# Weighting the routed rows of a mixture-of-experts layer before the down product, and adding them by the gathers

## The reference, cut to what matters

```python
xn = _layernorm(x)
scores = softmax(xn @ gate_w.T)                        # 64 experts
topk_w, topk_ids = top_k(scores, 6)                    # normalised to sum 1
comb = zeros(T, 64).at[token, topk_ids].add(topk_w)
g, u = split(einsum('th,efh->tef', xn, w_gate_up))     # 176 each
act = silu(g) * u * comb[:, :, None]
routed = einsum('tef,ehf->th', act, w_down)
shared = (silu(xn @ sg) * (xn @ su)) @ ws_down         # 2 shared experts
out = x + attention(xn) @ Wo + bo + routed + shared
```

## Time and profile before

| | |
|---|---|
| three runs | 660.39, 662.77, 664.65 us; median 662.77 |
| the profiled execution | 666.26 us, its span 664.4, mean granted clock 0.997 |
| busy in the span | PE 625.2 us (94%), DVE 437.2 (66%), POOL 360.4 (54%), ACT 308.0 (46%) |
| DMA | 124.52 MB, mean 187 GB/s |

### The profile page before, as it was taken

The page is one execution under the profiler, slowest core; times in us unless marked ns, Lnnn a source line. Parts: engine busy times, 40 slices in busy tenths (PEclk is TensorE's granted clock), DMA queues, the critical chain, the costliest instruction groups (busy, mean ns, idle before and its releaser), DMA issues.

```text
span 664.4 us, 17821 instructions
## 1 busy us (share of the span) xinstructions
PE 625.2 (94%) x4928; PEld 368.9 (56%) x4929; DVE 437.2 (66%) x1328; ACT 308.0 (46%) x798; POOL 360.4 (54%) x376
## 2 busy tenths in 40 slices
PE   6999999988989999899999989999999999999997
PEld 3644455654455555555555555555554666666654
DVE  6768678456474766656566575654446688898864
ACT  3653121033343444444444444454445767777752
POOL 3000000278685877868787686874300766666662
PEclk9999999999899999999999999999999999999999
DMA  8600011238869789796887969987425777777432
GB/s 272 189 32 1 0 34 33 94 95 269 264 183 264 243 250 286 211 325 200 261 281 228 307 198 298 286 251 163 98 58 190 213 217 228 221 219 222 130 103 74
DMA packets 78167, 124.52 MB, mean 187 GB/s; under 512 B 11113, under 2 KB 52618, under 8 KB 78090
## 3 DMA queue, kind: packets, MB, share of 16 engines
q1 hardware_dynamic: 43098, 60.18, 29.4%
q0 software_dynamic: 15872, 46.16, 24.5%
q10 hardware_dynamic: 19120, 17.18, 7.7%
HBM read 85.73 MB, written 37.75 MB: 186 GB/s over the span
## 4 chain that ended last, share of the span: by engine, by line
PE 78%; DVE 5%; issue 4%; ACT 4%; POOL 3%; DMA 3%; ACTq 2%; SPq 0%; DVEq 0%; POOLq 0%
PE pair L1181 22%; PE pair L1208 15%; PE pair L1151 6%; PE pair L1138 4%; PE pair L1086 4%; PE bank L1293 4%; PE bank L1192 3%; PE bank L1165 3%; PE bank L1325 2%; PE pair L1048 2%; DVE negm L950 2%; ACTq L616 2%; PE pair L1248 2%; PE pair L1267 1%; PE bank L1304 1%
## 5 line engine op out<-in xcount | busy, mean ns | idle before, releaser
L453 POOL DMA_INDIRECT lower<-xn_rows,idx_all x128 | 134.0, 1047 | 194.8 <-DVE idx_all L925 107.2
L1181 PE MATMUL pair<-space,work 128*64 (+1 forms) x768 | 167.3, 466 | 12.0 <-ACT work L601 7.6
L1208 PE MATMUL pair<-lower,work 88*64 x512 | 123.1, 380 | 5.2 <-ACT lower L614 2.7
L1181 PEld LDWEIGHTS pair<-space,work 128*64 128x64 f32 x768 | 67.4, 138 | 84.6 <-issue 63.4
L869 DVE TENSOR_TENSOR work<-work,pair 128x176 f32<-128x176 f32 x128 | 42.5, 337 | 105.2 <-ACT work L608 104.4
L1208 PEld LDWEIGHTS pair<-lower,work 88*64 88x64 f32 x512 | 68.7, 136 | 55.5 <-issue 22.6
L1181 PE MATMUL pair<-wqkv_sb,work 128*64 128x352 f32 x256 | 90.6, 477 | 0.0
L614 ACT ACTIVATE lower<-pair 128x256 f32<-128x256 f32 x128 | 49.2, 384 | 79.7 <-PE pair L1208 79.7
L518 POOL DMA_INDIRECT wqkv_sb<-y_rows,slot_i x48 | 47.2, 984 | 60.9 <-DVE negm L950 34.0
L601 ACT ACTIVATE work<-pair 128x256 f32<-128x256 f32 x128 | 42.4, 381 | 69.0 <-PE pair L1138 39.9
L950 DVE TENSOR_REDUCE negm<-pair 128x2 f32<-128x256 f32 (+1 forms) x128 | 64.9, 551 | 11.4 <-PE pair L1256 10.2
(11 more groups left out here) (198 smaller groups left out, 1199.8 us busy)
## 6 DMA issues: line engine op xcount, KB each, us to landing
space<-wgu SPq DMA_DIRECT2D x66, 352.0 KB
y_rows<-lower ACTq DMA_DIRECT2D x128, 128.0 KB, 4.0
qk_all<-qk_rows SPq DMA_DIRECT2D x64, 256.0 KB, 4.2
lower<-wdn SPq DMA_DIRECT2D x64, 176.0 KB
qk_rows<-qk_all POOLq DMA_DIRECT2D x32, 256.0 KB
qk_rows<-space POOLq DMA_DIRECT2D x16, 256.0 KB
xn_rows<-qk_all SPq DMA_DIRECT2D x16, 128.0 KB, 2.0
lower<-xn_rows,idx_all POOLq DMA_INDIRECT x128
```

Source lines behind the costliest of these rows:

```text
L453: po.indirect_dma_start(xg[:, r % XB, :], None, xn_rows[:, :], bass.IndirectOffsetOnAxis(idx_all[:, r:r + 1], 0)).then_inc(xg_in[r % XB], 16)
L1181: last = pe.matmul(pair[u % 2][strip, 0:2 * F], xgT[u][:, c, strip], n, start=c == 0, stop=c == EC - 1, skip_group_check=True)
L1208: last = pe.matmul(pair[u % 2][strip, 512:512 + E], hT[:, u % 2, c, strip], n, start=c == 0, stop=c == 1, skip_group_check=True)
```

## The change

A row's weight is applied to the hidden values of its tile, before the down product, instead of to its result afterwards. The rows of `xn_rows` become 64 columns wider; SP writes the token's 64 weights (`comb`, one for each expert) into these columns, and a gather brings 320 columns instead of 256. `take_weights` on DVE copies, for a tile, each strip's column of the gathered weights into one column of `wcol`: it loads the first strip's expert number into a register, waits for the gather, and makes one copy of 64 x 1 for each strip. The column then scales the rows in `hidden`, which becomes a scalar_tensor_tensor. A gather now also waits until the tile four before has had its weights taken.

`slot_weights`, `w6`, `combine` and the buffers `yg` go. In the attention POOL's gathers add into `x_all` themselves (`compute_op=ALU.add`): 96 as before, in groups of four token tiles, k by k; each waits for the add before it on the same tile (`summed`). `residual` waits for the adds of its two token tiles.

```diff
-    xn_rows = nc.dram_tensor("xn_rows", (T, E), F32, kind="Internal").ap()
+    xn_rows = nc.dram_tensor("xn_rows", (T, E + NE), F32, kind="Internal").ap()
...
+            sp.wait_ge(comb_ok, 1)
+            sp.dma_start(xn_rows.rearrange("(t p) e -> p t e", p=P)[:, :, E:E + NE], comb[:]).then_inc(comb_out, 16)
...
                 if r >= XB:
                     po.wait_ge(xt_done, r - XB + 1)
+                    po.wait_ge(taken, r - XB + 1)
...
-            def rows(t, u):
...
-                    if t >= 2:
-                        po.wait_ge(dcomb, TOPK * (t - 2) + k + 1)
-                    po.indirect_dma_start(yg[u][:, k, :], None, y_rows[:, :],
-                                          bass.IndirectOffsetOnAxis(slot_i[:, t, k:k + 1], 0)).then_inc(yg_in[u], 16)
+            def add_rows(t, k, paced):
...
+                before = t // GATHERED * TOPK + k
+                if before:
+                    po.wait_ge(summed[t % GATHERED], 16 * before)
+                po.indirect_dma_start(x_all[:, t], None, y_rows[:, :], bass.IndirectOffsetOnAxis(slot_i[:, t, k:k + 1], 0),
+                                      compute_op=ALU.add).then_inc(summed[t % GATHERED], 16)
...
-                dve.tensor_tensor(hid[:, u % 2], sg[:, u % 2], pair[u % 2][:, F:2 * F], ALU.mult).then_inc(hid_ok, 1)
...
+                dve.wait_ge(taken, i + 1)
+                dve.scalar_tensor_tensor(hid[:, u % 2], sg[:, u % 2], wcol[:, i % WEIGHTS:i % WEIGHTS + 1], pair[u % 2][:, F:2 * F],
+                                         ALU.mult, ALU.mult).then_inc(hid_ok, 1)
...
+            def take_weights(i, u):
+
+                dve.reg_load(low_reg[u], tile_e[0:1, 0, bass.ds(i, 1)])
+                dve.wait_ge(xg_in[u], 16 * (i // XB + 1))
+                for g, e in enumerate((dve.snap(low_reg[u], min_val=0, max_val=XT - 1) & (P - 1), own_of(u))):
+                    strip = slice(g * GRAIN, (g + 1) * GRAIN)
+                    last = dve.tensor_copy(wcol[strip, i % WEIGHTS:i % WEIGHTS + 1], xg[strip, u, bass.ds(e + (E - SHARED), 1)])
+                last.then_inc(taken, 1)
...
             for i in range(2):
                 up_copy(i, i)
+            for i in range(XB):
+                take_weights(i, i)
...
-                if 0 <= i // 2 < PAIRS * NT:
-                    slot_weights(i // 2)
+                for n in (i + XB, i + XB + 1):
+                    if XB <= n < TILES:
+                        take_weights(n, n % XB)
...
-                dve.wait_ge(dcomb, TOPK * SB * (b + 1))
+                for t in range(SB * b, SB * (b + 1)):
+                    dve.wait_ge(summed[t % GATHERED], 16 * TOPK * (t // GATHERED + 1))
```

More of the change, by code:

```diff
@@ L60 @@
 AHEAD = 9
+WEIGHTS = 16
+GATHERED = 4
 FILL = AHEAD + 2
@@ L203, in build @@
         npad = sb("npad", [P, SB, P])
-        w6 = sb("w6", [P, NT, 8])
+        wcol = sb("wcol", [P, WEIGHTS])
         cnt = sb("cnt", [NE, 1])
@@ L275, in build @@
         tiled = sem("tiled"); placed = sem("placed"); passed_ok = sem("passed_ok"); ended = sem("ended")
-        tables_ok = sem("tables_ok"); onehot_ok = sem("onehot_ok"); listed = sem("listed"); idx_ok = sem("idx_ok"); dpair = sem("dpair")
+        tables_ok = sem("tables_ok"); onehot_ok = sem("onehot_ok"); listed = sem("listed"); idx_ok = sem("idx_ok"); comb_ok = sem("comb_ok"); comb_out = sem("comb_out"); taken = sem("taken")
         w_loaded = [sem("w_loaded_even"), sem("w_loaded_odd")]
@@ L293, in build @@
         ot_ok = sem("ot_ok"); ot_taken = sem("ot_taken"); wo_ok = sem("wo_ok"); res_ok = sem("res_ok")
-        yg_in = [sem("yg_in0"), sem("yg_in1")]; dcomb = sem("dcomb")
+        summed = [sem(f"summed{u}") for u in range(GATHERED)]
         out_done = sem("out_done")
@@ L506, in _ @@
             assert done == todo
-            def rows(t, u):
[L510 to L515, removed]
-                    if t >= 2:
-                        po.wait_ge(dcomb, TOPK * (t - 2) + k + 1)
-                    po.indirect_dma_start(yg[u][:, k, :], None, y_rows[:, :],
-                                          bass.IndirectOffsetOnAxis(slot_i[:, t, k:k + 1], 0)).then_inc(yg_in[u], 16)
+            def add_rows(t, k, paced):
+                slot = ROWS_FROM + paced * NS // (TOPK * NT)
+                if slot < 0:
+                    po.wait_ge(max_ok, slot + AHEAD + 1)
+                else:
+                    po.wait_ge(exp_done, slot + 1)
+                before = t // GATHERED * TOPK + k
[3 more added lines that the diff above has]
+                                      compute_op=ALU.add).then_inc(summed[t % GATHERED], 16)
             po.wait_ge(dn_ok, TILES)
@@ L523, in _ @@
                 po.wait_ge(y_out[s], 16 * (RT // XB))
[L524 to L528, removed]
+            for n in range(TOPK * NT):
+                g, k, t = n // (TOPK * GATHERED), n // GATHERED % TOPK, n % GATHERED
+                add_rows(GATHERED * g + t, k, n)
         @block.scalar
@@ L886, in load_own @@
                 dve.reg_load(own_reg[u], tile_e[0:1, 1, bass.ds(i, 1)])
+            low_reg = [dve.alloc_register(f"low{u}") for u in range(XB)]
+            def take_weights(i, u):
[5 more added lines that the diff above has]
+                last.then_inc(taken, 1)
             def own_of(u):
@@ L999, in d_slot @@
                     maxes(n + AHEAD)
-                sums = []
-                first = n - LATER - (1 if n == NS + 2 else 0)
-                if 0 <= first and n - LATER < NS and n != NS + 1:
-                    sums = list(range(first * TOPK * NT // NS, (n - LATER + 1) * TOPK * NT // NS))
-                for i in sums[:1 if n < NS else 0]:
-                    combine(i)
                 if n % 2 == 0 and 0 <= n // 2 - 2 < QUADS:
@@ L1011, in d_slot @@
                     residual((n - 13) // 8)
-                for i in sums[1 if n < NS else 0:]:
-                    combine(i)
-            dve.wait_ge(dpair, PAIRS * NT)
             for u in range(BUFS):
```

26 lines of the change are left out of this document (4 added, 22 removed).

## The result

The changed kernel takes 801.99 us in the median of 4 runs (792.73 to 805.4), the kernel before 662.16 (4 runs): 1.206 times as long, with an interval of 1.201 to 1.210. (The ratio compares fast runs, so it leaves out the one of 805.4 us, which was in the slower state.) The prediction was 788.3, in a range of 704 to 830. The profiled execution took 804.04 us, its span is 802.2; against that of before, 666.26, it is 137.8 us longer.

A forecast was written before the change was run, and what follows sets the result against it. PE was taken to bound loop and attention, with DVE taking its place in the loop after the change: 666.26 + 94.5 (takes) + 3.4 (start) - 3.4 (attention) + 31 (clock) = 791.8, less 3.5 to the median: 788.3, range 704 to 830.

The forecast's parts named there:

- the two signs of being wrong: What would refute the prediction: a loop turn under 6 us, or an attention that grows.
- The loop's reading: Expert loop, undisturbed turn: PE needs 5.27 us, DVE's way from pair start through up_copy 4.25, so DVE is 1.02 ahead.
- The load, 0.63: Register load in each take on DVE's queue: 0.515 median plus 0.115, 0.63 us; bounds 0.297 and 0.955.
- The other seven instructions, 0.74: Rest of a take on DVE's queue, register work, waits and two one-column copies: 0.74 us, bounds 0.41 and 0.88.
- My 7.17: Forecast loop turn: 2.98 + 2.74 for two takes + 0.74 + 0.71 = 7.17 us against 5.67, +94.5 us over 63 turns.
- The clock, +31: Expert loop: PE's granted clock falls in a third of the turns, 21 x 1.48 = +31 us.
- The start, +3.4: Start of the loop: four takes, 5.5 us, before the first hidden, less 2.1 us DVE had there: +3.4 us.
- The attention, -3.4 for npad: Attention: with combines gone from DVE, seven of PE's eight waits before L1310 go, about 0.48 us each: -3.4 us.
- The adding gathers, "I take 0.98 for them too": Attention: each adding gather takes POOL 0.98 us, like the plain gathers it replaces.
- The rival with the slow adds: Attention: adds at twice 0.98 us plus 0.3 make POOL the pace, up to +67, 855 us; decides from 1.57 an add; chance 0.05.
- The residual's lateness, 4 us at most: Attention: last adds of every second batch may land 1 us late for the residual, 4 us in all at most; counted 0.
- Gathers as the bound: Rival in the loop: take, gather, landing and rotation bind at 6.2 us a turn if takes are cheap, about 697; chance 0.05.

The follow-up runs named there:

- the two mended versions: Changed kernel, takes ahead of hidden, both strips' expert numbers packed into the one number DVE loads anyway: 716.6 us; the same with the attention of before: 671.7 us.
- the experiment on it: Kernel before, with the two steps that fill npad ahead of that slot's combine instead of behind it: 663.1 us against 662.9, ratio 0.9995.

## Why the prediction was right, and where only its sum was

The time lies in the range, and the mechanism that carries it is shown: takes between hidden and up_copy make DVE the bound of the loop; without them the loop is back at 5.61 us a turn, and moved by a few lines they cost a fifth. But that the total came so near is luck: two errors offset each other. The loop was forecast 125.5 us longer (94.5 for the takes, 31 for the clock) and is 97.4 longer; the attention was forecast 3.4 shorter, and is 41.2 longer. An attention that grows was one of the two signs of being wrong that the prediction itself named, and it came.

- **The loop's reading** (PE 1.02 us ahead, DVE's way 4.25): right. The 1.11 us more of an undisturbed turn are what is left of two takes and one more thing, below, behind that slack. PE's waits before the up products are 1.2 us a turn, not 1.9.
- **The load, 0.63**: mis-sized. It costs 0.35 in an undisturbed turn. I took its price from the rows of L886, and these loads were quicker in every run with a turn of 7 us or more (0.30 in the median, also for L877, the old load under its new number; 0.47 in the two mended versions, at 5.78). The lower bound, 0.297, was the right end. The floor of about 600 ns that the Trainium skill states ("DMA: Bandwidth & Descriptors", section "Latency and other measured facts") does not hold for these.
- **The other seven instructions, 0.74**: 0.85 for a whole take less 0.35 leaves 0.50, nearer to the sum of durations (0.41) than to the value chosen between the bounds. That sum leaves out the two copies, 0.15 each, but the register rows of a take are shorter than the 0.11 that it has for each (0.05 to 0.07).
- **A term that was missing**: the 0.4 us from the end of the up_copy to the first product of the pair. In the turn that I read PE was not waiting for the copy, so it was hidden; once PE waits it is in the loop. The trace of before had it: in 21 of its 64 pairs PE stood still until 0.40 to 0.43 us after that copy. So of the 1.02 us that DVE was ahead, only 0.6 could be used up. With it, and takes at 0.85, the sum is 2.99 + 0.64 + 0.85 + 0.94 + 0.53 + 0.43 = 6.38, the undisturbed turn (0.64 to the first take's copies, 0.94 from the second's to the up_copy). My 7.17 was meant as a mean, with the clock's 31 us on top of it (7.66). That it is near the mean of 7.22 is luck: the undisturbed turn is 0.6 shorter than I reckoned, and the disturbances are larger than the 0.18 that I had put into the copy.
- **The disturbances**, 0.84 us a turn over 6.38: the clock up to 0.25 by the stretched pairs, the rotation about 0.2, the loads' tail about 0.3 by the estimate above. The parts need not add up, as one wait covers another, and only the rotation's is shown by a change of time (14 us over 63 turns).
- **The clock, +31**: it fell, as forecast, for 55 us of the loop (from the window's 0.94); what it cost can't be told from nothing, and the stretched pairs alone would put it at some 16.
- **The start, +3.4**: mis-sized with the take. The four takes there are 0.83 apart, and the first hidden comes at 139.23, 3.30 behind the first pair, against 138.47 - 136.68 = 1.79 in the earlier trace rows: 1.5 us.
- **The attention, -3.4 for npad**: the wait went, the time did not: 1.2 us in the experiment on it and 1.1 in that with plain gathers, both too little to tell.
- **The adding gathers, "I take 0.98 for them too"**: the step that failed. They take 1.54. The rival with the slow adds had the mechanism and a price (up to +67, measured +41 to +42), and I gave it 0.05. Its point of decision, 1.57 us an add, pause included, took the whole window of 150.4 us; the gathers of before had 137.6 us for 95 steps, so it is 1.45, against 1.84 measured. Nothing in the trace showed such a DMA, so the bound that I named should have had more weight than the nearest row.
- **The residual's lateness, 4 us at most**: I reckoned with the landing of the last add and not with a queue of adds behind the slots' pace; it was 36 us of PE's time.
- **Gathers as the bound**: not in the changed kernel, as forecast. It is what is left (10.6 us) where the takes are mended.

## What to carry to other kernels

An engine's in-order queue between two semaphores of a loop is a price list of its own: register loads and waits that no busy time shows cost as much there as the work, and the same instructions a few rows earlier, where the engine waits anyway, may be nearly free. Work taken off an engine that is not the bound returns nothing, and the instruction that replaces it has to keep the pace of its new engine: multiply its duration, with the pause before the next one, by its count, and set that against the stage. And when a new wait takes over a loop, add the latency from its releaser to the first work behind it, which was hidden until then.

## What the runs showed of the hardware

- An indirect gather of 128 rows of 256 columns that adds into SBUF kept POOL for 1.541 us and landed 4.8 us after its issue (median); the same without the adding kept it for 0.946.
- A register load on DVE's queue took 0.515 us in the median in the kernel before and 0.303 in the changed one, at a DMA share of 0.76 and 0.64 over the loop. Why is not shown.
- From the end of a DVE copy to the first product that waited for it, PE needed 0.40 us in most cases, and up to 0.56 (55 pairs).
- A DVE copy of 88 x 512 that takes 0.42 us took up to 2.2 while POOL ran its rotations, and the mean fell from 0.91 to 0.53 (the copy into `wqkv_sb`) when these were cut short.
